# A graph network kernel: its start and end reordered, and the transposes moved between two banks of gathers

## What is computed

```python
def layer0(x, adj, W1, b1, W2, b2):
    mask = (adj > 0.0)
    W1a, W1b = W1[:F], W1[F:]
    diff = x[:, :, None, :] - x[:, None, :, :]
    h = relu((x @ W1a)[:, :, None, :] + diff @ W1b + b1)
    hm = einsum('bjkh,bjk->bjh', h, mask)
    deg = sum(mask, axis=-1)
    return hm @ W2 + deg[..., None] * b2

def layer1(vertices, g_mat, W):
    agg = einsum('bnm,bmf->bnf', g_mat, vertices)
    return einsum('bnf,of->bno', agg, W)

x = x + layer0(relu(layernorm(x)), adj, W1, b1, W2, b2)
x = x + layer1(relu(layernorm(x)), adj, W)
```

## Time and profile before

| | |
|---|---|
| median of 3 runs | 842.6 us |
| the profiled execution | 845.98 us, span 844.1 us, granted clock 0.980 |
| PE, DVE, ACT, POOL busy | 810.6, 809.9, 794.9, 611.5 us |
| L414 with one-hots, 4096 matmuls | 417.0 us |
| L826, sums of the banks, 1024 | 559.7 us |
| L572, seeds, 1024 | 466.6 us |
| start of PE's first L456 (graph 0) | 56.23 us |
| start of the last L456 (graph 127) | 821.68 us |

### The profile page before, as it was taken

One profiled execution on the slowest core, in us unless ns is written; L12 is line 12 of the kernel. 1 busy time (PEld: TensorE's weight loads), 2 busy tenths in 40 slices (PEclk: granted clock), 3 DMA queues, 4 the chain that ended last, 5 costly groups with the idle time before them and its releaser, 6 DMA issues.

```text
span 844.1 us, 26648 instructions
## 1 busy us (share of the span) xinstructions
PE 810.6 (96%) x8242; PEld 715.0 (85%) x8243; DVE 809.9 (96%) x2894; ACT 794.9 (94%) x2246; POOL 611.5 (72%) x1174
## 2 busy tenths in 40 slices
PE   4879999999999999999999999999999999999996
PEld 2447888898889888988998899888988898889884
DVE  6969999999999999999999999999999999999993
ACT  4969999999999999999999999999999999999992
POOL 1966777777777777777777777777777777777762
PEclk8979999999999999999999999999999999999996
DMA  9800000000000000000000000000000000000000
GB/s 337 327 1 2 7 9 21 21 21 15 21 20 21 9 21 21 20 15 21 21 21 9 20 21 21 15 21 20 21 9 21 21 20 14 21 21 21 15 3 21
DMA packets 26705, 27.55 MB, mean 33 GB/s; under 512 B 3520, under 2 KB 24512, under 8 KB 25536
## 3 DMA queue, kind: packets, MB, share of 16 engines
q1 hardware_dynamic: 25488, 25.37, 8.9%
q10 hardware_dynamic: 1072, 0.43, 0.2%
HBM read 21.59 MB, written 4.19 MB: 31 GB/s over the span
## 4 chain that ended last, share of the span: by engine, by line
PE 90%; DVE 4%; issue 2%; ACT 2%; DMA 1%; SPq 0%; ACTq 0%; DVEq 0%
PE ring L414 48%; PE ring L442 8%; PE prep L471 5%; PE post L514 4%; PE post L501 3%; PE post L508 3%; PE post L502 3%; PE prep L479 3%; PE prep L482 2%; PE prep L477 2%; DVE acc L826 2%; PE post L506 2%; DMA x_all<-x_nbf_dram 1%; PE prep L473 1%; DVE onehot_space L812 1%
## 5 line engine op out<-in xcount | busy, mean ns | idle before, releaser
L826 DVE SCALAR_TENSOR_TENSOR acc<-ring,acc 128x384 f32<-128x384 f32 x896 | 488.6, 545 | 0.6
L572 ACT COPY ring<-P 128x384 f32<-128x384 f32 x1024 | 466.6, 509 | 19.3 <-DVE acc L826 11.4
L414 PE MATMUL ring<-PQ,onehot_space 128*128 128x192 f16 x4096 | 417.0, 247 | 4.5 <-ACT ring L572 2.2
L414 PEld LDWEIGHTS ring<-PQ,onehot_space 128*128 128x128 f16 x4096 | 328.0, 99 | 39.4 <-issue 13.5
L922 POOL TENSOR_SCALAR start<-P,spare 128x192 f32<-128x192 f32 x128 | 128.4, 1003 | 134.8 <-ACT P L622 133.8
L946 POOL TENSOR_TENSOR row_space<-row_space 128x192 f32<-128x192 f32 x256 | 153.4, 599 | 25.3 <-ACT row_space L610 8.2
L812 DVE TENSOR_SCALAR onehot_space<-mask_all 128x512 f16<-128x512 f16 x512 | 158.1, 311 | 0.0
L442 PE MATMUL ring<-PQ,owner 128*128 128x384 f16 (+1 forms) x512 | 93.9, 306 | 0.0
L414 PE MATMUL ring<-PQ,onehot_row 128*128 128x192 f16 x768 | 84.3, 246 | 0.5 <-DVE onehot_row L874 0.3
L610 ACT ACTIVATE row_space<-ring 128x576 f32<-128x576 f32 x128 | 83.3, 651 | 0.7 <-PE ring L414 0.7
L826 DVE SCALAR_TENSOR_TENSOR acc<-ring,start 128x384 f32<-128x384 f32 x128 | 71.1, 556 | 5.3 <-PE ring L414 1.3
(11 more groups left out here) (138 smaller groups left out, 1431.9 us busy)
## 6 DMA issues: line engine op xcount, KB each, us to landing
onehot_space<-adj_kbj_dram SPq DMA_DIRECT2D x8, 1024.0 KB, 17.3
adj_again<-adj_kbj_dram SPq DMA_DIRECT2D x128, 64.0 KB, 2.0
x_all<-x_nbf_dram SPq DMA_DIRECT2D x8, 512.0 KB, 19.0
out_dram<-x_all SPq DMA_DIRECT2D x32, 128.0 KB, 1.9
consts<-consts_dram SPq DMA_DIRECT2D x1, 192.0 KB, 2.4
scratch<-w1a_dram ACTq DMA_DIRECT2D x2, 48.0 KB, 4.2
scratch<-w1b_dram ACTq DMA_DIRECT2D x2, 48.0 KB, 6.7
scratch<-b_dram ACTq DMA_DIRECT2D x1, 96.0 KB, 10.1
```

The lines of the kernel that those rows point to most:

```text
L414: last = nc.tensor.matmul(to, hot(s), parts[:, part, H:2 * H], start=False, stop=(part == 1), skip_group_check=True)
L572: return nc.scalar.copy(slots[to][:, bank_], src.unsqueeze(1).broadcast_to([N, PER_BANK, H]))
L826: return nc.vector.scalar_tensor_tensor(sums, slots[to][:, bank_], 0.0, start[:, :, :] if first else sums, ALU.max, ALU.subtract if first ...
```

## The change

- PE: the block of i == 3 becomes a function `across`. In steps with gathers it is called between the first and the second bank of the fourth chunk. Its wait for the row sums stands behind the transposes of L501.
- ACT: ownerT's copy goes behind the first seed of the fourth chunk. The copy of code_row gets a semaphore of its own, which DVE's L874 waits for.
- Start: PE does parts 1 to 3 whole, the search's matmuls behind parts 2 and 3; DVE's largest, largest_of_rows, scale and second_parts come a part or more later; ACT makes L654 behind part 4 and the two first steps of `lead`. PE writes four banks of the ring before it sums the rows; ACT seeds behind that, and waits for the others in the third chunk. DVE makes the first four compares before the codes are all there and two more before `fits`; the first second_part goes behind the fits. POOL's start sums no longer wait for the tables.
- POOL: the last power (32 graphs) is cut into four pieces of 8, at the ends of the steps 3, 5, 7 and 9. ACT waits for them in step 11 instead of step 8.
- End: the row sums of the last graph are made by DVE in step 128. ACT makes both h2 of a pair in one step. The last four graphs are stored by two DMAs.

```diff
         @block.sync
-            sp.wait_ge(y_ready, B // 2)
-            sp.dma_start(out[:, B - STORE:B, :], x_all[:, B - STORE:B, :]).then_inc(stored, 16)
+            for done in range(B - STORE + 2, B + 1, 2):
+                sp.wait_ge(y_ready, done // 2)
+                sp.dma_start(out[:, done - 2:done, :], x_all[:, done - 2:done, :]).then_inc(stored, 16)
...
         @block.tensor
             codes(0)
-            codes(1, range(QUADS // 2))
+            codes(1)
+            codes(2)
             pe.wait_ge(largest_ready, 1)
...
-            codes(1, range(QUADS // 2, QUADS))
+            codes(3)
             pe.wait_ge(largest_ready, 2)
...
-            with pe.Fori(2, LATE) as g:
+            with pe.Fori(EARLY, LATE) as g:
...
+            def across(b, u, looped, t):
+                main = exists(b)
+                last = None
+                if main:
+                    pe.wait_ge(rows_ready, b + 1)
+                if exists(b + 2):
+                    pe.wait_ge(h1_split, b + 3)
+                    last = nc.tensor.matmul(h1T_ps, ...)
+                if exists(b - 1):
+                    pe.wait_ge(summed, b * REGULAR)
+                    for s in range(PER_BANK):
+                        nc.tensor.matmul(head_ps, acc_space[...], ident, start=(s == 0), stop=False, is_transpose=True)
+                    pe.wait_ge(hm_row_ready, b)
+                    last = nc.tensor.matmul(head_ps, row_heads[(u - 1) % 2], ownerT[...], start=False, stop=True)
...
                                 gather(dst, parts, hot).then_inc(gathered, 1)
+                                if i == 3 and bank_ == 0:
+                                    across(b, u, looped, t)
...
-                    if i == 3:
-                        ...
-                        if last:
-                            last.then_inc(transposed, 1)
+                    if i == 3 and not main:
+                        across(b, u, looped, t)
...
-            pe.wait_ge(rows_counted, 1)
-            nc.tensor.matmul(tables[:, 0, :], ones[:, :], rows, start=True, stop=True)
-            nc.tensor.matmul(tables[:, 1, :], rows, ones[:, :], start=True, stop=True).then_inc(rows_summed, 1)
             pe.wait_ge(code_kj_ready, B // QUAD)
-            pe.wait_ge(code_jk_ready, B // QUAD)
-            write_ring(range(QUADS))
+            write_ring(range(QUADS)).then_inc(ring_ready, 1)
+            pe.wait_ge(rows_counted, 1)
+            nc.tensor.matmul(tables[:, 0, :], ones[:, :], rows, start=True, stop=True)
+            nc.tensor.matmul(tables[:, 1, :], rows, ones[:, :], start=True, stop=True).then_inc(rows_summed, 1)
...
         @block.scalar
+                        if i == 2 and isinstance(b, int) and b == 0:
+                            act.wait_ge(ring_ready, 2)
...
                             seed(place(u, i), P[:, u % 2, :], bank_).then_inc(seeded, 1)
+                            if i == 3 and bank_ == 0:
+                                nc.scalar.copy(ownerT[:, u % QUAD, :], ownerT_ps).then_inc(rows_ready, 1)
...
-                        nc.scalar.copy(code_row[:, :], code_row_ps)
-                        nc.scalar.copy(ownerT[:, u % QUAD, :], ownerT_ps).then_inc(rows_ready, 1)
+                        nc.scalar.copy(code_row[:, :], code_row_ps).then_inc(code_row_ready, 1)
...
             codes(0)
-            codes(1)
-            codes(2)
+            with nc.scalar.Fori(1, EARLY) as g:
+                codes(g)
+            codes(EARLY)
+            act.wait_ge(norm1_ready, 1)
+            lead(step, hi=-1)
             act.wait_ge(scale_ready, 1)
             nc.scalar.activation(w_parts[:, 0, :, 0:H], ...).then_inc(first_parts_ready, 1)
-            codes(3)
-            act.wait_ge(norm1_ready, 1)
-            lead(step, hi=-1)
-            with nc.scalar.Fori(EARLY, PARTS) as g:
+            with nc.scalar.Fori(EARLY + 1, PARTS) as g:
                 codes(g)
...
-            act.wait_ge(tables_ready, 1)
             act.wait_ge(ring_ready, 1)
...
         @block.vector
             norm1_stats(1)
+            mask(2)
             largest()
-            mask(2)
-            largest_of_rows()
             moments(0)
             norm1_stats(2)
-            scale()
             mask(3)
+            largest_of_rows()
             norm1_stats(3)
             moments(1)
             mask(4)
-            second_parts()
+            scale()
             mask(5)
             norm1_stats(4)
+            second_parts()
             mask(6)
...
             moments(3)
+            dve.wait_ge(code_kj_ready, 1)
+            first_hot()
...
-            dve.wait_ge(p_ready, 1)
-            second_part(0, 0)
+            hot(0, 0, 1, 0)
+            hot(0, 0, 1, 1)
...
+                if not main and b == B:
+                    dve.wait_ge(relu_row_ready, B)
+                    sums = relu_rows[(u - 1) % 2][:, 0, :]
+                    nc.vector.tensor_tensor(sums, sums, relu_rows[(u - 1) % 2][:, 1, :], ALU.add).then_inc(half_row_ready, 1)
+                    dve.wait_ge(half_row_ready, B)
+                    nc.vector.tensor_tensor(sums, sums, relu_rows[(u - 1) % 2][:, 2, :], ALU.add).then_inc(hm_row_ready, 1)
...
-                        dve.wait_ge(rows_ready, b + 1)
+                        dve.wait_ge(code_row_ready, b + 1)
...
         @block.gpsimd
+            def last_norm1(k):
+                piece = GROUP * PER_PART // PIECES
+                b = slice(B - (PIECES - k) * piece, B - (PIECES - k - 1) * piece)
+                nc.gpsimd.tensor_tensor(rstd1[:, b], mom[:, 3, b], half_power[:, :].broadcast_to([N, piece]),
+                                        ALU.pow).then_inc(pool_step, 1)
+                pool.wait_ge(pool_step, GROUPS + k)
+                nc.gpsimd.tensor_tensor(shift1[:, b], mom[:, 0, b], rstd1[:, b], ALU.mult).then_inc(norm1_ready, 1)
...
-                if exists(b - 1):
+                if exists(b - 1) and exists(b):
                     pool.wait_ge(relu_row_ready, b)
...
+                if isinstance(b, int) and b % 2 and b // 2 in range(1, PIECES + 1):
+                    last_norm1(b // 2 - 1)
...
-            pool.wait_ge(tables_ready, 1)
             pool.wait_ge(p_ready, 1)
             start_sums(0, 0)
             lead(step, lo=-1)
-            norm1(GROUPS - 1)
+            some = load_any(nc.gpsimd)
```

119 lines of the change are left out of this document (62 added, 57 removed).

## The result

Fifteen runs each, on the same chip: the changed kernel has a median of 846.18 us (844.65 to 848.56), the kernel before 843.8 (842.23 to 845.79). The ratio is 1.003, 95% interval 1.0018 to 1.0041. I had forecast 837.5, with 844 as the upper end. The three runs that the forecast started from had a median of 842.6, so 1.2 us of the miss lie in the starting point and the rest in the parts: 2.4 us slower in place of some 5 to 6 us faster.

The account below looks back on a forecast made before the run. A ring of waits through PE, DVE and ACT was taken to set the loop's pace. -6.0 + 1.8 - 1.5 - 0.7 = -6.4 us gave 839.6 or 836.2, taken as 837.5; range 831.5 to 844.

Parts of the forecast that it names:

- The loop: PE's block between the fourth chunk's banks and ownerT's later copy: -6.0 us, ends 0 and -11.
- the ring gets 0.24 us shorter: Loop: cycle of waits through PE, DVE and ACT over four graphs shortens, saving 0.06 us a graph.
- DVE takes the relief: Rival, loop: DVE's compares or sums are late wherever PE comes sooner; -1 instead of -6, 841.5 us; chance 0.24.
- The slower rival: Rival, loop: POOL's row sums arrive late between the banks and PE stands in each pair; 847 us, chance 0.12.
- two slacks of 0.3 us and less: Loop: 0.3 us left before odd graphs' row sums, 0.34 before DVE's compares' gathers with 0.24 eaten.
- The pieces: POOL's last power in four parts, graphs 4 to 10: +0.45 us each, +1.8 in all, ends 0 and +4.
- DVE, behind by its 2 us, feels a part: Pieces: PE stalls about 1.1 us for row sums; DVE's lag passes on only some, +0.45 us a piece.
- The lock rival: Rival, pieces: each piece holds DVE for its length, 6.8 us in place of 1.8; 842.5 us, chance 0.05.
- The head: Start, up to the first graph: -1.1 + 0.6 - 1.6 = -2.1, taken as -1.5 us, ends -4 and +1.
- the wait ahead of second_parts: Head: DVE stands before second_parts from about 30.8 to 33.2, about 2.4 us.
- The last code copy: Head: ACT's final copy of the codes ends at about 45.2 us.
- The tail: Behind the last row gather: row sums on DVE let L502 start 0.7 us sooner; -0.7 us, 0 to -1.5.

Follow-up runs that it names:

- a_onepower: The changed kernel with POOL's last power again in one piece, ahead of step 0: 842.21 us, ratio 0.9952.
- a_tailpool: The changed kernel with the last graph's row sums on POOL again: 848.0 us, ratio 1.0015.
- d_tailwait: The changed kernel with, only behind the last graph, the row-sum wait again ahead of the head's two transposes: 845.71 us, ratio 1.0022.
- e_loop: The kernel before plus only the loop's part: PE's block between the banks, row-sum wait behind transposes, ownerT's copy between seeds: 842.13 us, ratio 0.9981.
- e_onepower: The same kernel as a_onepower, run again on another chip: 843.86 us, ratio 1.0002.
- f_looptail: The kernel before plus the loop's and the tail's part of the change, neither head nor pieces: 841.41 us, ratio 0.9968.
- a_blockback: The changed kernel with PE's block again behind both banks of the fourth chunk, ACT's order as changed: 848.45 us, ratio 1.0025.
- e_pieces: The kernel before plus only POOL's last power in four pieces, in steps 3, 5, 7 and 9: 847.94 us, ratio 1.0045.
- e_oneback: The changed kernel with the power in one piece ahead of step 0 and PE's block behind both banks of chunk four: 845.32 us, ratio 1.0016.
- f_tail: The kernel before plus only the tail's part of the change: 842.06 us, ratio 0.9977.
- a_rowslast: The changed kernel with the row-sum wait and its matmuls at the very end of PE's block, head sums differing: 842.86 us, ratio 0.9958.
- c_both: The changed kernel with one power ahead of step 0 and, in odd steps, adjacency matmuls ahead of the head's: 842.40 us, ratio 0.998.
- c_dveminus: Meant to drop a VectorE compare from c_both, but its condition left nothing out, so the same kernel again: 841.79 us, ratio 0.998.

## Why the forecast missed

**The loop (forecast -6.0, in the traces about -0.3).** Seven traces have the new order from graph 14 to 127 and no other edit there (after, a_onepower, a_tailpool, d_tailwait, e_loop, e_onepower, f_looptail: 680.30 to 683.03, mean 681.4), five the old one (before, a_blockback, e_pieces, e_oneback, f_tail: 680.49 to 683.64, mean 681.7). (In a_blockback and e_oneback ScalarE's copy keeps its new place.) The step that failed is "the ring gets 0.24 us shorter" as a gain of time. The ring was read rightly as a chain of waits, and relief of nearly the size forecast did reach VectorE: its stands ahead of a graph's first sum are 8.4 to 10.0 us in the five traces of the old order (mean 9.2) and 1.8 to 8.3 in the seven of the new (mean 4.8). But VectorE then meets POOL's work at other moments, and its held compares go from 13.5 to 16.0 us (mean 14.7) to 14.6 to 21.6 (mean 18.9). So 4.4 us of waits become 4.2 us of holds, and the rest of the balance stays as it was. No run keeps the holds of the old order while the block moves; that the holds eat the relief is read from these twelve balances.

It was "DVE takes the relief" (chance 0.24) that came nearest, with the right place, VectorE's compares, but a wrong reason for doubting it: that VectorE "mostly follows" because it waits for TensorE once a graph. Those waits fall to 1.5 us in a_rowslast and the period stays. The slower rival, row sums late between the banks, did appear (6.0 us of waits, 3.8 of them away from the pieces), because two slacks of 0.3 us and less were booked as free; the loop of a_rowslast, without these waits, is no shorter than before.

**The pieces (forecast +1.8, ends 0 and +4; alone +3.8).** Place and length were right, and the wait of 0.85 us in the block is near the estimated 1.1. What failed is "DVE, behind by its 2 us, feels a part": in the graphs 4 to 12 the even intervals grow to 7.45, 7.27, 7.03 and 7.04 us, by 0.8 to 1.0 each, and VectorE shows it as a wait for TensorE (0.75 us at 87.30). The forecast used the lag for the sum right behind the block; VectorE's own stand comes three us later. How much a piece costs also hangs on where TensorE waits for the row sums: with that wait last, in a_rowslast, the graphs 0 to 14 take 2.0 us less. The lock rival had 6.8 us for the four pieces and is out: no piece holds VectorE's compare up, as the row at 80.90 shows.

**The head (forecast -1.5; graph 0 0.2 us sooner, by the ratios below +3 or -1.4).** Term by term it was good where a row backed it: the wait ahead of second_parts (2.64 for 2.4). The last code copy was not. It was laid out for 45.2 and ends at 46.6, since ScalarE still stands for TensorE and the masks, 1.2 us twice:

```profile
18.88 0.59 ACT L576 CAST mask_all<-ring 128x512 f32 x1 [1.23 <-PE ring L394]
...
24.11 0.59 ACT L576 CAST mask_all<-ring 128x512 f32 x1 [1.22 <-PE ring L394]
```

Graph 0 then begins at 56.0 and not at 54.7. The clock has a part in it too. From the last code copy to graph 0 it is 9.4 us with a granted clock of 0.68 between 46 and 56 us (after), and 8.0 us in c_both and c_dveminus, where that clock was 0.95 and 0.99 and graph 0 began at 54.1 and 54.7. What the head does give with one power (graph 0 at 54.1 to 55.9, in five executions) it mostly loses again at once: the first three graphs take 19.3 to 19.7 us with the new head and one power, 17.9 to 19.0 with the new head and four pieces, 18.4 to 18.7 with the old head and either. The long power of the new head ends as step 1 begins, and POOL and VectorE then stand for each other (e_onepower):

```profile
55.71 5.79 POOL L966 TENSOR_TENSOR rstd<-mom,half_power 128x32 f32<-128x32 f32 x1
...
62.56 0.93 POOL L954 TENSOR_SCALAR start<-P,spare 128x192 f32<-128x192 f32 x1 [0.73 <-DVE acc L854]
...
63.52 0.56 DVE L854 SCALAR_TENSOR_TENSOR acc<-ring,start 128x384 f32<-128x384 f32 x1 [1.62 <-POOL start L954]
```

At graph 14 the new head with one power stands at 139.2 to 142.3 us, the old one at 140.1 to 141.2. Why the old head doesn't pay this was not tried and stays open, and so does what the head is worth.

**The tail (forecast -0.7; -3.0 in the trace, -1.9 us alone).** The term left out TensorE's clock, which the traces show. In the kernel before, TensorE stands 1.87 us ahead of 829.44, and behind that the granted clock is at half:

```profile
831.29 0.77 PE L477 MATMUL prep<-w2b,sums_T 128*128 128x128 f32 x2 [0.55 <-ACT sums_T L604]
...
831.00:841.00 10.00, 7.27 (x24) 5.56 (x24) 1.75 (x8) 2.39 (x8) 1.32 (x4) 0.50 0.06 18
```

The same matmuls take 0.46 us after (835.19, above), and in f_tail the clock of that stretch is 0.91:

```profile
831.00:841.00 10.00, 3.73 (x22) 2.61 (x21) 1.75 (x8) 2.24 (x7) 1.32 (x4) 0.91 0.12 34
```

Two edits each do it. The longest stand of TensorE in the 10 us behind graph 127, and what lies behind that graph, are 1.87 and 22.42 us in the kernel before, 1.86 and 22.10 in e_pieces. With the wait behind the transposes, which cut the stand in two, they are 1.32 and 19.51 (e_loop), 1.32 and 19.83 (a_tailpool). With VectorE's sums and the wait ahead 1.08 and 18.67 (d_tailwait), with both 0.77 to 1.06 and 18.4 to 19.4 (after, f_looptail, f_tail). So it jumps by 2.3 us between 1.86 and 1.32 and moves by 1.5 us below, not in the order of the stands. That the stand is what lowers the clock fits these eight traces and wasn't tried alone. It can't be the stand alone: with the same stand of 0.77 us the clock fell 11.2 us behind graph 127 in after and 14.7 behind in f_looptail. Each kernel has one trace, and the 21 to 27 executions of the kernel before in each group had mean granted clocks from 0.978 to 0.991. In group f its eight executions at 0.981 or less took 845.06 us on average, the fourteen at 0.984 or more 843.95. The traced one had 0.980 and lay 2 us above the median. So part of the 3.0 us may lie in which execution of the kernel before was traced, and the 1.9 us of the medians are the better figure.

**The sum.** By the runs of single parts: pieces +0.45%, loop and tail -0.32%, and the changed kernel at +0.30% leaves +0.17%, 1.4 us, for the head and the way the parts meet. By e_oneback less f_tail the head is +3.3 us, by e_onepower less f_looptail +2.9, all four on one chip; by a_onepower, from another chip, less f_looptail it is -1.4. So on the one chip where it can be read it cost some 3 us, and over both chips its sign is not settled.
